# Mixture-of-experts stage: 39 tiles of 256 rows become 32 of 256 and 8 of 128 rows

## The reference, cut to what matters

```python
w_gate = transpose(gating_einsum)          # [E, 512, 2 * 512]
gate_out = ragged_dot(sorted_xs, w_gate, group_sizes=tokens_per_expert).reshape(n, 2, H)
activation = gelu(gate_out[:, 0, :]) * gate_out[:, 1, :]
expert_outputs = ragged_dot(activation, linear, group_sizes=tokens_per_expert)
```

## Time and profile before

| | us |
|---|---|
| median of 3 runs (3730.55 to 3732.28) | 3731.57 |
| the profiled execution | 3731.69 |
| its span, first to last instruction | 3729.9 |
| PE busy in the span | 3581.6 (96%) |
| DVE busy | 2182.2 (59%) |
| ACT busy | 1822.4 (49%) |
| POOL busy | 1531.7 (41%) |

### The profile page before, as it was taken

One profiled execution on the slowest core, in us unless ns is written; L12 is line 12 of the kernel. 1 busy time (PEld: TensorE's weight loads), 2 busy tenths in 40 slices (PEclk: granted clock), 3 DMA queues, 4 the chain that ended last, 5 costly groups with the idle time before them and its releaser, 6 DMA issues. The chain is left out here.

```text
span 3729.9 us, 68005 instructions
## 1 busy us (share of the span) xinstructions
PE 3581.6 (96%) x23268; PEld 3103.4 (83%) x23268; DVE 2182.2 (59%) x5411; ACT 1822.4 (49%) x4698; POOL 1531.7 (41%) x1536
## 2 busy tenths in 40 slices
PE   7999999999999998699999997999999899999999
PEld 7999999999999997699999985666666578877777
DVE  6666666556666665566666676777777542222221
ACT  4444445544444443455555544777777632222222
POOL 3333333534444443465566644766666430000000
PEclk9999999999999999899999998999999899999999
DMA  4566665316666661666666652221221120000000
GB/s 153 177 224 222 228 224 214 126 57 218 217 217 217 217 224 51 234 240 227 239 233 240 231 189 94 67 64 60 65 64 61 40 82 23 23 23 23 23 23 23
DMA packets 227766, 520.16 MB, mean 139 GB/s; under 512 B 12273, under 2 KB 28914, under 8 KB 223474
## 3 DMA queue, kind: packets, MB, share of 16 engines
q1 hardware_dynamic: 122866, 296.36, 22.8%
q10 hardware_dynamic: 94432, 187.71, 13.6%
q0 software_dynamic: 10272, 33.63, 2.7%
HBM read 266.52 MB, written 251.13 MB: 139 GB/s over the span
## 5 line engine op out<-in xcount | busy, mean ns | idle before, releaser
L672 POOL TENSOR_SCALAR a_prob<-a_prob,a_rinv 128x256 f32<-128x256 f32 x512 | 471.3, 931 | 836.0 <-DVE a_rinv L855 836.0
L619 ACT ACTIVATE a_prob<-a_prob,a_low_bias 128x256 f32<-128x256 f32 x512 | 256.5, 502 | 458.6 <-DVE a_low_bias L846 458.6
L1118 PE MATMUL e_gb<-e_xt_hi,in_hi 128*128 128x256 f32 x1248 | 354.5, 284 | 5.7 <-DVE e_xt_lo L1244 5.7
L1120 PE MATMUL e_gb<-e_xt_hi,in_lo 128*128 128x256 f32 x1248 | 354.4, 284 | 0.0
L1102 POOL TENSOR_TENSOR e_act_hi<-e_act_f,e_zeros 128x256 fp32r<-128x256 f32 x156 | 234.6, 1504 | 285.3 <-DVE e_act_f L1264 273.7
L1119 PE MATMUL e_gb<-e_xt_lo,in_hi 128*128 128x256 f32 x1248 | 351.5, 282 | 0.0
L2242 ACT ACTIVATE f_h_f<-f_hb,b_sb 128x512 f32<-128x512 f32 x128 | 88.1, 688 | 478.3 <-PE f_hb L2180 414.4
L422 PE MATMUL a_pj<-a_xt,a_wq_hi 128*128 128x256 f32 x1024 | 310.2, 303 | 0.9 <-DVE a_q_lo L705 0.9
L424 PE MATMUL a_pj<-a_xt,a_wq_lo 128*128 128x256 f32 x1024 | 289.4, 283 | 0.0
L423 PE MATMUL a_pj<-a_xt,a_wq_hi 128*128 128x256 f32 x1024 | 289.0, 282 | 0.0
L705 DVE TENSOR_TENSOR a_ot_lo<-a_avb,a_ot_hi 128x256 fp32r<-128x256 f32 x256 | 108.3, 423 | 254.4 <-ACT a_ot_hi L624 254.4
(11 more groups left out here) (362 smaller groups left out, 11370.7 us busy)
## 6 DMA issues: line engine op xcount, KB each, us to landing
raw_in<-in_w_gate SPq DMA_DIRECT2D x39, 2048.0 KB, 7.8
x_sorted<-a_blank ACTq DMA_DIRECT2D x42, 1792.0 KB, 6.5
y_sorted<-a_blank ACTq DMA_DIRECT2D x42, 1792.0 KB, 8.5
raw_out<-in_w_out SPq DMA_DIRECT2D x39, 1024.0 KB, 5.1
e_xg<-x_sorted SPq DMA_DIRECT2D x39, 512.0 KB, 8.4
y_sorted<-e_y_sb SPq DMA_DIRECT2D x39, 512.0 KB, 2.8
xt_rows<-a_xt SPq DMA_DIRECT2D x16, 1024.0 KB, 5.1
a_xt<-xt_rows SPq DMA_DIRECT2D x16, 1024.0 KB, 5.2
```

The costliest lines, as they stand in the source:

```text
L619: e = nc.scalar.activation(prob[:, u % 4, t], prob[:, u % 4, t], ACT.Exp, bias=low_bias[:, u % 2, t:t + 1], scale=-1.0, accum_out=rsum[:, ...
L672: p = nc.gpsimd.tensor_scalar(prob[:, u % 4, t], prob[:, u % 4, t], rinv[:, u % 2, t:t + 1], None, ALU.mult)
L1118: nc.tensor.matmul(out, a_hi, b_hi, start=start, stop=False)
L1120: return nc.tensor.matmul(out, a_lo, b_hi, start=False, stop=stop)
```

## The change

Lists are rounded up to 128 rows instead of 256. A fixed schedule of 40 tiles runs: tiles 2, 7, 12, ..., 37 (8 of them) have 128 rows, the other 32 have 256. The first part of each list goes to tiles of 256 rows, an odd remainder of 128 rows to a small tile; the table has 31 rows for large tiles (tile 0 is fixed) and the rest for small ones.

In a small tile the operands change place. `gate_up_rows` lets 128 rows of x stand in the array and streams 512 columns of gate weights: 2 x 4 x 3 matmuls into two whole PSUM banks. The result is rows by hidden units, so gelu and product are one instruction each over 512 elements, and four transposes (`turn_rows`) bring the activations back into the form that `down` wants, in `gb[2]`. ACT and DVE read them there to make high and low half (`turned_rows`); POOL has nothing to do for a small tile. The loops over pairs of tiles are written out, tile by tile, on all engines.

```diff
-TILES = TOK * TOPK // TILE + E - 1
+PAIR_TILES, HALF_TILES = TOK * TOPK // TILE - 1, E
...
+    FULL = [n % 5 != 2 for n in range(1 + PAIR_TILES + HALF_TILES)]
+    LAST = len(FULL) - 1
...
+            def gate_up_rows(n):
+                b = buf(n)
+                pe.wait_ge(xt_lod, 2 * n + 4)
+                pe.wait_ge(in_lod, FC * (n + 1))
+                for k in range(2):
+                    pe.wait_ge(act_done, HC * n + k + 1)
+                    for c in range(FC):
+                        w = slice(k * H0, (k + 1) * H0)
+                        mm = three(gb[k][:], xt_hi[:, b, c, 0:P], xt_lo[:, b, c, 0:P], in_hi[:, b, c, w], in_lo[:, b, c, w], c == 0, c == FC - 1)
+                    mm.then_inc(g_ready, HC // 2)
+
+            def turn_rows(n):
+                pe.wait_ge(act_done, HC * (n + 2))
+                for h in range(HC):
+                    mm = nc.tensor.transpose(gb[2][:, h * P:(h + 1) * P], act_row[:, h * P:(h + 1) * P], ident[:])
+                mm.then_inc(row_turned, 1)
...
-            with pe.Fori(0, TURNS - 1) as i:
-                for b in range(2):
-                    n = 2 * i + b
-                    gate_up(n + 1, 1 - b)
-                    turn(n + 2, b, i + 2)
-                    down(n, b)
+            for n in range(1, LAST):
+                if FULL[n]:
+                    gate_up(n)
+                else:
+                    gate_up_rows(n)
+                turn(n + 1)
+                down(n - 1)
+                if not FULL[n]:
+                    turn_rows(n)
...
+            def tile_rows(n):            # on ACT
+                in_high(n + 1, 0)
+                in_high(n + 1, 1)
+                act.wait_ge(g_ready, HC * n + HC // 2)
+                act.wait_ge(act_done, HC * (n + 1))
+                nc.scalar.activation(gelu_row, gb[0][:], ACT.Gelu_apprx_tanh).then_inc(gelu_done, HC)
+                in_high(n + 1, 2)
+                in_high(n + 1, 3)
+                turned(n + 1)
+                for h in range(HC):
+                    out_high(n, h)
...
+            def tile_rows(n):            # on DVE
+                for q in range(3):
+                    in_low(n + 1, q)
+                dve.wait_ge(gelu_done, HC * (n + 1))
+                dve.wait_ge(g_ready, HC * (n + 1))
+                dve.wait_ge(act_lod, HC * n + 2)
+                nc.vector.tensor_tensor(act_row, gb[1][:], gelu_row, ALU.mult).then_inc(act_done, HC)
+                in_low(n + 1, 3)
+                turned(n + 1)
+                for h in range(HC):
+                    out_low(n, h)
+
+            def turned_rows(n):          # on DVE, after ACT's high half
+                b = buf(n)
+                dve.wait_ge(row_hid, FULL[0:n + 1].count(False))
+                low(act_lo[:, b, :, 0:P], gb[2][:].rearrange("p (h s) -> p h s", h=HC), act_hi[:, b, :, 0:P]).then_inc(act_lod, HC)
```

More of the change, by code:

```diff
@@ L942, in _ @@
[L942 to L947, removed]
@@ L1039, in fetch, with load_x @@
[L1039 to L1043, removed]
+            def load_x(n, place):
+                b, t = buf(n), rows_of(n) // P
+                sp.dma_start(xg[:, b, 0:t], x_sorted[place, :].rearrange("(t p) d -> p t d", p=P)).then_inc(x_loaded[b], 16)
@@ L1044, in fetch @@
+            def fetch(n):
+                e = bass.ds(sp.value_load(table[0:1, 2 * ROW[n]:2 * ROW[n] + 1], min_val=0, max_val=E - 1), 1)
+                place = bass.ds(sp.value_load(table[0:1, 2 * ROW[n] + 1:2 * ROW[n] + 2], min_val=0, max_val=SLOTS - TILE), rows_of(n))
+                if n > 1:
                     sp.wait_ge(in_lod, FC * (n - 1))
                     sp.nop(nofuse=True)
-                load_in(b, e)
-                if not (isinstance(n, int) and n == 1):
+                load_in(buf(n), e)
+                if n > 1:
@@ L1063, in _ @@
             sp.wait_ge(tab_loaded, 16)
-            fetch(1, 1)
-            fetch(2, 0)
-            with sp.Fori(0, TURNS - 1) as i:
-                for b in range(2):
-                    fetch(2 * i + b + 3, 1 - b)
-                    store(2 * i + b, b)
+            fetch(1)
+            fetch(2)
+            for n in range(LAST - 2):
+                fetch(n + 3)
+                store(n)
             sp.wait_ge(in_lod, FC * LAST)
@@ L1108, in _ @@
             pool.wait_ge(zeros_set, 1)
-            split(0, 0)
-            with pool.Fori(0, TURNS) as i:
-                for b in range(2):
-                    n = 2 * i + b
-                    split(n + 1, 1 - b)
+            for n in range(LAST + 1):
+                if FULL[n]:
+                    split(n)
         @block.tensor
@@ L1136, in gate_up @@
                     pe.wait_ge(act_done, HC * n + h + 1)
+                    if h == 2 and n and not FULL[n - 1]:
+                        pe.wait_ge(act_lod, HC * (n + 1))
                     for k in range(2):
@@ L1147, in down @@
                 pe.wait_ge(out_lod, FC * (n + 1))
-                for t in range(TT):
+                for t in parts(n):
                     for h in range(HC):
@@ L1205, in last_tile, with gelu_of @@
-            def last_tile(n, b, count):
-                for h in range(HC):
[L1207 to L1210, removed]
+            def gelu_of(n, h):
+                act.wait_ge(g_ready, HC * n + h + 1)
+                act.wait_ge(act_done, HC * n + h + 3)
+                nc.scalar.activation(gelu[:, h % 2], gb[h][:, 0:TILE], ACT.Gelu_apprx_tanh).then_inc(gelu_done, 1)
@@ new lines, in tile @@
+            def tile(n):
+                for h in range(HC):
+                    gelu_of(n, h)
+                    in_high(n + 1, h)
+                    out_high(n, h)
[9 more added lines that the diff above has]
+                turned(n + 1)
+                for h in range(HC):
+                    out_high(n, h)
@@ L1221, in _ @@
             for q in range(FC):
-                in_high(0, 0, q, 1)
-            turned(0, 0)
-            tile(0, 0, 1)
-            with act.Fori(0, TURNS - 1) as i:
-                for b in range(2):
-                    n = 2 * i + b
-                    tile(n + 1, 1 - b, i + 1 + b)
-                    rows_of_y(n, b, i + 1)
-            tile(LAST - 1, 1, TURNS)
-            rows_of_y(LAST - 2, 0, TURNS)
-            last_tile(LAST, 0, TURNS + 1)
+                in_high(0, q)
+            turned(0)
+            tile(0)
+            for n in range(1, LAST):
+                if FULL[n]:
+                    tile(n)
+                    rows_of_y(n - 1)
+                else:
+                    tile_rows(n)
+                    rows_of_y(n - 1)
+                    turned_rows(n)
+            last_tile(LAST)
             act.wait_ge(after_loaded[3], 16)
@@ new lines, in gated, with tile @@
+            def gated(n, h):
+                dve.wait_ge(gelu_done, HC * n + h + 1)
+                dve.wait_ge(act_lod, HC * n + h + 1)
+                nc.vector.tensor_tensor(act_f[:, h], gb[h][:, TILE:], gelu[:, h % 2], ALU.mult).then_inc(act_done, 1)
+            def tile(n):
+                for h in range(HC):
+                    gated(n, h)
+                    in_low(n + 1, h)
+                    out_low(n, h)
+                turned(n + 1)
+            def tile_rows(n):
[6 more added lines that the diff above has]
+                in_low(n + 1, 3)
+                turned(n + 1)
+                for h in range(HC):
+                    out_low(n, h)
@@ L1320, in _ @@
             for q in range(FC):
-                in_low(0, 0, q)
-            turned(0, 0)
-            tile(0, 0)
-            with dve.Fori(0, TURNS - 1) as i:
-                for b in range(2):
-                    tile(2 * i + b + 1, 1 - b)
-            tile(LAST - 1, 1)
+                in_low(0, q)
+            turned(0)
+            tile(0)
+            for n in range(1, LAST):
+                if FULL[n]:
+                    tile(n)
+                else:
+                    tile_rows(n)
+                    turned_rows(n)
             for n, name in enumerate(("wkv", "wd")):
```

228 lines of the change are left out of this document (136 added, 92 removed).

## The result

The changed kernel takes 3691.13 us (median of 4 runs, 3690.09 to 3691.93) against 3731.63: a ratio of 0.9891, with a 95% interval of 0.9875 to 0.9907. It is 40.5 us faster; the forecast was 35.7. The profiled execution took 3691.33 us, its span is 3689.6.

What follows compares the result with a forecast made beforehand. PE was taken to bound the mixture stage. Large tiles -124.9, small tiles +72.8, stalls behind them +14.4 and the table +2.0 gave -35.7 from the profiled 3731.69, so 3696.0 us, range 3689 to 3704.

Steps and rivals of the forecast that it cites:

- Tiles: PE in the mixture: 7 large tiles of 17.85 us fewer (-124.9), 8 small ones of 9.1 us own work (+72.8).
- The stall behind a small tile: Large tile after a small one: PE waits 1.8 us for operands, as halved `down` covers less; eight times, +14.4 us.
- The operands of tile n+1 in the small tile: Small tile: ACT and DVE finish the next tile's halves at 11.6 us, PE wants them at 12.2; no stall, 0.
- The rival in which conversions become the bound: DVE's chain in small tiles slips behind PE at both places by about 1.5 us more: 3720 us, chance 0.06.
- The table: Table chain after its matmul: 16 links instead of 10, 4.1 us instead of 2.07, so +2.0 us.
- Nothing covers this: End of the first function: the barrier follows the table's store, so the longer chain's +2.0 us shifts the first loads too.
- The ends of the stage: First and last tile: same code, hanging on the same relative times, so 0, with 2 us either way.
- First tiles: Start of the stage: the first tile's code and relative times unchanged, so 0, with 2 us either way.
- lower the clock: Rival: eight new PE stalls each bring the slow clock, 1.4 us apiece, +11; 3704 to 3715 with double stalls, chance 0.14.
- Fetches: Rival: exposed instruction fetches of written-out loops, 35 packets at 1.02 us, take the whole gain, up to 3742; slower 0.05.
- That the change doesn't pay at all: No gain or a loss, by fetches or something unseen in the unrolled order: chance 0.09, of which slower 0.05.
- The range: Forecast time of the whole kernel, from bounds that can go both ways: 3689 to 3704 us, chance 0.68.

Runs made afterwards that it cites:

- a longer table: The kernel before with 10 more links in the table's chain, each adding zero to one column: 3730.3 us beside 3729.69.
- the early load: The kernel before, with SP asking for the next attention's wq and wo ahead of storing tile LAST-2's result: 3727.22 us against 3731.2, ratio 0.9990.
- POOL's sums from SBUF: The changed kernel, with POOL making six unused SBUF-to-SBUF sums of 128x256 elements in each small tile: 3692.12 us.

## Why the prediction was right, and where it was off

*Tiles.* Right: 17.85 us for a large one, and a small one's own work: 12.31 us from start to start against 12.2. `turn_rows` took 0.36 instead of 0.4, a matmul over 512 columns of gate weights 0.234 instead of 0.229.

*The stall behind a small tile.* The place, the cause and the count are right: the experiment that takes `e_wo_lo` out of the chain takes 1.14 us out of the stall. The size was 1.8 and measured 1.37. Start to start the sum holds (16.78 against 16.9). DVE's chain (tile start 1653.52) ends as forecast, 16.7 us behind the start:

```profile
1668.96 1.28 DVE L1339 TENSOR_TENSOR e_xt_lo<-e_tb,e_xt_hi 128x512 fp32r<-128x512 f32 x2
```

PE begins 0.06 us after it, not 0.2. PE's own work is 15.25 from start to start (11.59 + 0.79 + 2.87), not 15.1, which leaves 1.53. The last 0.16 are a matter of counting: the profile counts idle time from the modelled end of the last matmul (0.39 us long), while the next would have started after 0.23. The tile after it took 18.0 instead of 17.85; the cause stays open. Over a cycle of five tiles the forecast was 82.3 us and the trace has 82.4.

*The operands of tile n+1 in the small tile.* "No stall, but with only 0.4 us to spare" had the right sign by a wrong step. I let ACT wait for both halves of the product; its gelu needs only the first, and the semaphore is raised by two after each half. In the trace gelu starts 3.06 us after the tile, not at 5.8 (ACT, then DVE, changed kernel):

```profile
1644.27 0.60 ACT L1287 ACTIVATE e_gelu<-e_gb 128x512 f32<-128x512 f32 x1
...
1648.94 1.28 DVE L1339 TENSOR_TENSOR e_xt_lo<-e_tb,e_xt_hi 128x512 fp32r<-128x512 f32 x2
```

The halves are ready 9.0 us after the start instead of 11.6: the slack is 3.3 us. The rival in which conversions become the bound stood only on that 0.4. The four `e_wo_lo` of a small tile took 0.68 us each, as forecast.

*The table.* The chain was sized right (1499.67 - 1495.50 = 4.17 us against 4.1) and put on the path wrongly. "Nothing covers this" failed: in the kernel before POOL held the barrier until 1.8 us after SP was ready. 0.7 us showed instead of 2.0. Another 0.2 is no part of it: the whole end of this function, POOL's DMAs too, ran 0.2 later in this execution.

*The ends of the stage.* "Hangs on the same relative times" failed. Tile LAST-2 is a small one now; its result is copied 0.7 us before the start of the last `gate_up`, not until 1.3 us behind it, so SP's store and the load behind it come earlier: -2.5 us. I had followed the queue of SP inside the loop, but not at its end.

*First tiles.* The slow clock at tile 1 lasted 6.8 us instead of 3.4 in this execution and took back 1.4. The window of the earlier trace rows, changed kernel:

```profile
1538.00:1545.00 7.00, 6.47 (x31) 6.47 (x32) 0.90 (x2) 0.95 (x2) 0.03 (x1) 0.52 0.93 272
```

Of the eight experiments' traces four have 3.4 at this place and four 6.8, and the kernel before is found on both sides (3.4 as it is and written out, 6.8 with a longer table and with the early load). So it need not be the change's. That the change makes the long one likelier isn't excluded: the three traces with its first tiles as they are all have 6.8, and the three others have a shorter wait or a small tile there. It is the larger part of why the stage won 36.5 and not 37.7.

*Rivals.* The stalls of 1.37 us didn't lower the clock: 1.00 over the window. Fetches are excluded by the written-out kernel before, and by this kernel's window, in which the stalls make up all idle time. That the change doesn't pay at all would have been true of its first half alone, the shorter lists with weights standing; the forecast had no separate term for that and took it from matmuls over 512 columns in the earlier trace rows.

Together: the span became 40.3 us shorter, the forecast said 35.7. Of the 4.6 between them, 1.3 come from the table, 2.5 from the load of wq and 2.3 from the two stretches after it; the stage takes back 1.2. That makes 4.9; the other 0.3 are the later end of the first function (0.2) and the stretch to the first `gate_up` (0.1). The 2.3 are chance, by the spread that these two stretches have over the ten traces; without them the distance to the forecast is 2.3 us.

*The range.* Its upper end was added up too low: the bounds that it names, +6.6 for the stall, +1.4 for the table and +2 for the ends, give 3706, not 3704. Nothing hangs on it here.

## What to carry to other kernels

Halving a block's rows halves PE's time only if the streaming side stays long: here 512 columns at 0.23 us, while 128 columns cost almost what 256 do. When blocks of two sizes alternate, the short one takes away the cover of its neighbour: find the chain that ended just ahead of PE, and order it so that what PE wants next comes first. At both ends of a stage, write down what the barrier and each load wait for; a chain that looks last may not be (0.7 of 2.3 us showed), and a store ahead of a load in one queue can cost more (3.6 us).

## What the runs showed of the hardware

In the mixture, a matmul with a weight load of its own followed another after 0.11 us at 128 columns, 0.12 at 256 and 0.23 at 512. PE's idle gaps of 1.37 us, eight in dense work, left the granted clock at its full level of 2.4 GHz; at the end of the gap at the first tiles, 3.0 to 4.3 us, it fell to 1.2 GHz in all ten traces. It stayed there for 3.4 us in five of them and for 6.8 in five, and the kernel before shows both with nothing changed at that place; it loses 1.4 us by the first and the changed kernel 2.8 by the second (20.26 instead of 17.44).

A DVE subtraction of 128x512 elements from two SBUF operands took 0.68 us, and 1.10 beside POOL's sums from SBUF, which then took 0.94; with one operand in PSUM it kept its 0.68, and the sum beside it took 0.61. At the barrier POOL reported 5.4 us after its last indirect DMA instruction had ended, in all ten traces.
